# One kernel, one change: the first double by eight plain products, with both of its convolutions first

## The reference

```python
out = lax.conv_general_dilated(x, weight, window_strides=(STRIDE,), padding=[(PAD, PAD)], dimension_numbers=('NCH', 'OIH', 'NCH'), feature_group_count=GROUPS)
ctx = jnp.einsum('nd,od->no', c, c_weight)
out = out + ctx[:, :, None] + bias[None, :, None]
...
w = kernel.astype(x.dtype) * 2.0 - 1.0
return scale * jnp.einsum('bsi,if->bsf', x, w)
...
x = x + _L0_ffn_ref(_L0_cond_ref(x, cond_128, L0_cond_weight, L0_cond_c_weight, fside_S_0), L0_ffn_kernel, L0_ffn_scale)
```

## Time and profile before

| | us |
|---|---|
| median of 3 runs | 186.67 (186.43 to 186.93) |
| the profiled execution | 187.07 |
| its span in the trace | 185.0 |
| outside the span | 2.07 |
| PE busy | 171.9 (93%) |
| DVE busy | 132.3 (72%) |
| ACT busy | 69.0 (37%) |

### The profile page before, as it was taken

How to read it: one execution, slowest core, us unless ns; L and a number is a source line. 1 busy time by engine, 2 the same in 40 slices (tenths; PEclk the granted TensorE clock), 3 DMA queues, 4 the chain that set the end, 5 groups by cost and what they waited for, 6 DMA issues and landing times.

```text
span 185.0 us, 2886 instructions
## 1 busy us (share of the span) xinstructions
PE 171.9 (93%) x1007; PEld 148.8 (80%) x1007; DVE 132.3 (72%) x196; ACT 69.0 (37%) x77; POOL 6.6 (4%) x16
## 2 busy tenths in 40 slices
PE   3899799588999999999999999999999999999892
PEld 0569599376898989898899889888989889987681
DVE  4434788999967596758767786768766876587762
ACT  3534722491726163514624190617260502023000
POOL 5213200000000000000000000000000000000000
PEclk9999999999999999999999999999999999999999
DMA  6789785628696768376937785678834760005005
GB/s 221 186 201 299 208 246 83 150 39 153 137 287 148 170 100 319 70 177 97 265 118 111 164 167 230 88 170 113 315 56 59 103 238 5 0 0 227 4 0 227
DMA packets 23854, 27.51 MB, mean 149 GB/s; under 512 B 2753, under 2 KB 19313, under 8 KB 23841
## 3 DMA queue, kind: packets, MB, share of 16 engines
q1 hardware_dynamic: 22896, 25.96, 56.5%
q0 software_dynamic: 304, 1.09, 2.4%
q10 hardware_dynamic: 640, 0.28, 0.7%
HBM read 10.47 MB, written 8.40 MB: 102 GB/s over the span
## 4 chain that ended last, share of the span: by engine, by line
PE 87%; DVE 4%; DMA 3%; issue 3%; ACT 1%; ACTq 1%; DVEq 0%
PE ps_A L628 30%; PE ps_conv L610 30%; PE ps_C L628 15%; PE ps_B L628 8%; DMA cw_nat<-c_weight 3%; PE ps_A L577 2%; DVE sums L459 1%; PE ps_toep L628 1%; PE ps_C L597 1%; DVE y_sum L442 1%; DVE sign_T L415 1%; ACT hi_S L362 1%; DVE x_nat L480 0%; DVE lo_S L467 0%; ACT hi_A L362 0%
## 5 line engine op out<-in xcount | busy, mean ns | idle before, releaser
L610 PEld LDWEIGHTS ps_conv<-toeplitz,x_blk 128*128 128x128 f32 x512 | 61.2, 196 | 3.0 <-issue 1.9
L610 PE MATMUL ps_conv<-toeplitz,x_blk 128*128 128x128 f32 x512 | 61.3, 280 | 1.2 <-DVE y_sum L442 1.2
L362 ACT CAST hi_S<-sums 128x512 fp32r<-128x512 f32 x32 | 19.1, 621 | 55.5 <-DVE sums L459 54.7
L442 DVE TENSOR_TENSOR y_sum<-ps_conv,shift 128x512 f32<-128x512 f32 (+1 forms) x33 | 22.1, 674 | 18.2 <-PE ps_conv L610 11.4
L480 DVE SCALAR_TENSOR_TENSOR x_nat<-ps_A,scale_col,x_nat 128x512 f32<-128x512 f32 x31 | 23.2, 750 | 12.2 <-PE ps_A L628 12.1
L349 ACT COPY x_phase<-x_nat 128x1032 f32<-128x1032 f32 x13 | 28.2, 2173 | 0.0
L362 ACT CAST hi_A<-y_sum 128x512 fp32r<-128x512 f32 x24 | 14.0, 617 | 34.7 <-DVE y_sum L442 34.7
L467 DVE TENSOR_TENSOR lo_S<-sums,hi_S 128x512 fp32r<-128x512 f32 x32 | 21.8, 683 | 0.8 <-ACT hi_S L362 0.8
L628 PE MATMUL ps_A<-sign_T,hi_S 128*128 128x512 f32 x64 | 18.6, 412 | 1.8 <-DVE x_nat L480 0.9
L628 PE MATMUL ps_A<-sign_T,lo_S 128*128 128x512 f32 x64 | 17.1, 389 | 0.0
L467 DVE TENSOR_TENSOR lo_A<-y_sum,hi_A 128x512 fp32r<-128x512 f32 x24 | 16.3, 682 | 0.4 <-ACT hi_A L362 0.4
(11 more groups left out here) (68 smaller groups left out, 153.9 us busy)
## 6 DMA issues: line engine op xcount, KB each, us to landing
x_nat<-x SPq DMA_DIRECT2D x16, 512.0 KB, 4.1
x_blk<-x_phase SPq DMA_DIRECT2D x123, 64.5 KB, 2.5
out<-x_nat SPq DMA_DIRECT2D x15, 512.0 KB, 5.3
w_bytes<-w_bool SPq DMA_DIRECT2D x2, 512.0 KB, 5.9
shift<-shift_dram POOLq DMA_DIRECT2D x1, 896.0 KB, 5.7
out<-x_nat SPq DMA_DIRECT2D x1, 256.0 KB, 2.9
out<-x_nat SPq DMA_DIRECT2D x2, 128.0 KB, 2.8
x_blk<-x_phase ACTq DMA_DIRECT2D x3, 64.5 KB, 3.8
```

Of the source, the lines that this page charges most:

```text
L362: nc.scalar.copy(hi[k][:, :, :], flat(operand(k))).then_inc(hi_ok[k], 1)
L442: nc.vector.tensor_tensor(y_sum[r][:, u, a, :].rearrange("m u a o -> m a u o"), ps_conv[:, a, u, :], shift_of(d, r, a).unsqueeze(2).to_bro ...
L610: now = nc.tensor.matmul(ps_conv[:, a].rearrange("m u o -> m (u o)"), x_blk[r][:, a, s:s + M], toeplitz[:, s, g].rearrange("r u o -> r u ( ...
```

## The change

The first double is computed by eight plain products (`PLAIN`), with no S and no T operand. Both its convolutions come ahead of them; the convolutions of the second double stand behind the fifth and the seventh (`CONV_AFTER`). A21 shares its tiles with S4 and B12 with T4; a fourth bank E is the one that the Toeplitz transposes used. The steps 1 to 7 are as before on PE; T4 is now made ahead of step 1. B21 is made on ACT in four pieces that are signalled one by one. The sign bytes are loaded behind the first blocks of both pairs, where the first half stood ahead of them. The blocks of pair 1 are issued by three queues instead of one. DVE spreads all of the taps, whose load is now the third on ACT's queue. The shift of the first eight batches is one matmul of ones against `early_rows`, behind the first half of `conv(0, 0)`. `WARM` is 10 at the start and 2 ahead of the convolution. (Steps that count doubles only change their count; they are left out below.)

```diff
-WARM = 4, 3, 4
+WARM = 10, 2
...
-FIRST_BLOCKS = {("SP", 0): (0, 1), ("ACT", 0): (2, 3), ("SP", 1): (4,), ("ACT", 1): (5,), ("POOL", 1): (6, 7)}
-EARLY = 4
+FIRST_BLOCKS = {("SP", 0): (0, 1), ("ACT", 0): (2,), ("POOL", 0): (3,), ("SP", 1): (4,), ("ACT", 1): (5, 6),
+                ("POOL", 1): (7,)}
+EARLY = 8
...
+PLAIN = (("A12", "B21", "A"), ("A12", "B22", "B"), ("A22", "B21", "C"), ("A22", "B22", "E"), ("A11", "B11", "A"),
+         ("A11", "B12", "B"), ("A21", "B11", "C"), ("A21", "B12", "E"))
+CONV_AFTER = {4: 0, 6: 1}
+LAST_USE = {"A12": 2, "A22": 4, "A11": 6, "A21": 8}
+PLAIN_SUMS = {"A": (0, 0), "B": (0, 1), "C": (1, 0), "E": (1, 1)}
+PLAIN_BANK = {"P2": "B", "P1": "A", "P5": "C"}
+PLAIN_DONE = {"A": 5, "B": 6, "C": 7, "E": 8}
...
+        hi["A21"], lo["A21"] = hi["S4"], lo["S4"]
...
+        signs["B12"] = signs["T4"]
...
+        bank["E"] = ps_last[:, 0]
...
+            first_blocks(sp, "SP", 0)
+            first_blocks(sp, "SP", 1)
             signs_in(sp, 0)
-            first_blocks(sp, "SP")
+            load(1, 0, x_first[2])
             signs_in(sp, 1)
-            load(1, 0, x_first[2])
-            to_blocks(0, 1)
             load(1, 1, x_first[3])
...
-            first_blocks(pool, "POOL")
+            first_blocks(pool, "POOL", 0)
+            first_blocks(pool, "POOL", 1)
...
-            act.dma_start(taps_nat[:, :, :], weight).then_inc(taps_in, 16)
             act.dma_start(cond_nat[:, :], cond).then_inc(small_in, 16)
             act.dma_start(cw_nat[:, :], c_weight).then_inc(small_in, 16)
+            act.dma_start(taps_nat[:, :, :], weight).then_inc(taps_in, 16)
...
-            act.wait_ge(taps_zero, 1)
-            act.wait_ge(taps_in, 16)
-            expand_taps(nc.scalar.copy, B // 2, B).then_inc(exp_ok, 1)
...
+            first_blocks(act, "ACT", 1)
+
+            def sign(k, pieces):
+
+                rows = 0 if k[1] == "2" else KH
+                f = int(k[2]) - 1
+                for piece in range(pieces):
+                    n = KH // pieces
+                    u = KH - n * (piece + 1)
+                    nc.scalar.activation(signs[k][:, u:u + n, :], w_bytes[:, rows + u:rows + u + n, f * BANK:(f + 1) * BANK],
+                                         ACT.Copy, bias=-0.5, scale=1.0).then_inc(sign_ok[k], n)
...
-            high_part("A12", 0)
-            high_part("A11", 0)
-            sign("B22", slice(0, KH), 1)
-            to_phases(1, 1)
-            high_part("S2", 0)
-            high_part("S1", 0)
-            doubles(step)
+            def first_double():
+
+                high_part("A12", 0)
+                act.wait_ge(w_in[0], 16)
+                sign("B21", KH)
+                sign("B22", 1)
+                high_part("A22", 0)
+                high_part("A11", 0)
+                act.wait_ge(w_in[1], 16)
+                sign("B11", 1)
+                to_phases(1, 1)
+                sign("B12", 1)
+                high_part("A21", 0)
+                to_phases(2, 0)
+                high_part("A12", 1)
+                high_part("A11", 1)
+                to_phases(2, 1)
+                high_part("S1", 1)
+                high_part("S2", 1)
...
+            nc.vector.memset(warm[:, :], 0.0).then_inc(warm_ok, 1)
...
+            for half in range(2):
+                expand_taps(nc.vector.tensor_copy, half * B // 2, (half + 1) * B // 2).then_inc(exp_ok, 1)
...
-            dve.wait_ge(toep_done, 2)
-            toeplitz_of(nc.vector.tensor_copy, 1).then_inc(toep_ok, 1)
             dve.wait_ge(x_first[1], 16)
             nc.vector.tensor_copy(x_phase[1][:, :, 0:M + 1],
                                   x_nat[:, 1, :].rearrange("r (m q) -> r q m", q=B)).then_inc(phase_ok[1], B)
+            dve.wait_ge(toep_done, 2)
+            toeplitz_of(nc.vector.tensor_copy, 1).then_inc(toep_ok, 1)
+            dve.wait_ge(ctx_done, 1)
             dve.wait_ge(bias_in, 16)
-            dve.wait_ge(ctx_done, 1)
-            nc.vector.tensor_tensor(shift_rows[:, :], ps_ctx, bias_rows[0:N, :], ALU.add).then_inc(shift_ok, 1)
+            nc.vector.tensor_tensor(shift_rows[:, :], ps_ctx, bias_rows[:, :], ALU.add).then_inc(shift_ok, 1)
+            dve.wait_ge(shift_ok, 1)
+            dve.wait_ge(ident_ok, 1)
+            nc.vector.tensor_tensor(early_rows[:, :, :], shift_rows[:, :].unsqueeze(1).to_broadcast([N, EARLY, C]),
+                                    ident[0:N, 0:EARLY].unsqueeze(2).to_broadcast([N, EARLY, C]), ALU.mult
+                                    ).then_inc(rows_ok, 1)
             dve.wait_ge(early_done, 1)
-            nc.vector.tensor_tensor(shift[:, 0:EARLY // 2].rearrange("m j a o -> m (j a o)").rearrange("m (n o) -> m n o", n=EARLY),
-                                    ps_early.rearrange("m (n o) -> m n o", n=EARLY),
-                                    bias_rows[:, :].unsqueeze(1).to_broadcast([P, EARLY, C]), ALU.add).then_inc(early_ok, 1)
+            nc.vector.tensor_copy(shift[:, 0:EARLY // 2].rearrange("m j a o -> m (j a o)"), ps_early).then_inc(early_ok, 1)
...
+            def plain_sum(b):
+
+                r, f = PLAIN_SUMS[b]
+                dve.wait_ge(plain_done, PLAIN_DONE[b])
+                there = line(0, r, *columns(f))
+                nc.vector.scalar_tensor_tensor(there, bank[b], scale2_col[:, :], there, ALU.mult, ALU.add
+                                               ).then_inc(plain_summed[b], 1)
+
+            def first_double():
+
+                LOW, HIGH = slice(0, KH // 2), slice(KH // 2, KH)
+                add_shift(0, 0, 0)
+                add_shift(0, 0, 1)
+                low_part("A12", 0)
+                add_shift(0, 1, 0)
+                add_shift(0, 1, 1)
+                dve.wait_ge(scale_in, 16)
+                nc.vector.tensor_scalar(scale2_col[:, :], scale_col[:, :], 2.0, 0.0, ALU.mult, ALU.add
+                                        ).then_inc(scale_ok, 1)
+                low_part("A22", 0)
+                low_part("A11", 0)
+                for half in range(2):
+                    dve.wait_ge(w_in[half], 16)
+                sign_sums("T3", w_bytes[:, 0:KH, BANK:L], ALU.subtract, w_bytes[:, KH:B, BANK:L])
+                low_part("A21", 0)
+                dve.wait_ge(sign_ok["T3"], KH)
+                dve.wait_ge(sign_ok["B11"], KH)
+                sign_sums("T2", plain("T3"), ALU.add, plain("B11"))
+                dve.wait_ge(scale_ok, 1)
+                plain_sum("A")
+                dve.wait_ge(sign_ok["T2"], KH)
+                dve.wait_ge(sign_ok["B22"], KH)
+                sign_sums("T1", plain("B22", LOW), ALU.subtract, plain("T2", LOW), LOW)
+                add_shift(1, 0, 0)
+                sign_sums("T1", plain("B22", HIGH), ALU.subtract, plain("T2", HIGH), HIGH)
+                add_shift(1, 0, 1)
+                plain_sum("B")
+                low_part("A12", 1)
+                plain_sum("C")
+                low_part("A11", 1)
+                add_shift(1, 1, 0)
+                add_shift(1, 1, 1)
+                for k in ("S1", "S3", "S2", "S4"):
+                    combine(k, 1)
+                plain_sum("E")
+                low_part("S2", 1)
+                dve.wait_ge(sign_ok["B21"], KH)
+                dve.wait_ge(plain_done, LAST_USE["A21"])
+                for u in (LOW, HIGH):
+                    sign_sums("T4", plain("B21", u), ALU.subtract, plain("T2", u), u)
...
-            for n in range(EARLY):
-                now = nc.tensor.matmul(ps_early[:, n * C:(n + 1) * C], cond_t[:, n:n + 1].to_broadcast([D, P]), cw_t[:, :],
-                                       start=True, stop=True)
-            now.then_inc(early_done, 1)
-            keep_busy(WARM[2])
+            keep_busy(WARM[1])
+
+            def early_shift():
+
+                pe.wait_ge(ones_ok, 1)
+                pe.wait_ge(rows_ok, 1)
+                nc.tensor.matmul(ps_early, ones[:, :], early_rows[:, :, :].rearrange("k n o -> k (n o)"),
+                                 start=True, stop=True).then_inc(early_done, 1)
...
+            def first_double():
+
+                for n, (of, k, b) in enumerate(PLAIN):
+                    pe.wait_ge(hi_ok[of], 1)
+                    opens = n < 4
+                    for part in (hi, lo):
+                        if part is lo:
+                            pe.wait_ge(lo_ok[of], 1)
+                        for u in range(KH):
+                            if part is hi:
+                                pe.wait_ge(sign_ok[k], u + 1)
+                            now = nc.tensor.matmul(bank[b], part[of][:, u, :], signs[k][:, KH - 1 - u, :],
+                                                   start=opens and u == 0 and part is hi,
+                                                   stop=not opens and u == KH - 1 and part is lo, skip_group_check=True)
+                    now.then_inc(plain_done, 1)
+                    if n in CONV_AFTER:
+                        conv(1, CONV_AFTER[n])
...
```

(18 more changed lines are left out.)

221 lines of the change are left out of this document (94 added, 127 removed).

## The result

The changed kernel takes 181.38 us in the median of 4 runs (180.59 to 181.48), the kernel before 186.80 us in the same comparison: ratio 0.9698, 95% interval 0.9663 to 0.9733. A second set of six runs gave 181.65 us (181.31 to 182.18), ratio 0.9736 (0.9710 to 0.9762). So the change is 3.0% or 2.6% faster, 5.2 to 5.4 us. The forecast was 179.8 us, the range 178.0 to 182.6.

The account below looks back on a forecast made before the run. PE bounds the kernel, with holes before step 1, where DVE's queue is tight. Step 1 at 40.5 + 0.4 + 0.3 = 41.2 instead of 48.07, 6.9 us less: 180.2 profiled, 179.8 median; range 178.0 to 182.6.

Parts of the forecast that it names:

- The case that it rested on: Whole kernel: the prediction's own sum, 179.8 us, holds within 0.8 us; chance 0.45.
- the sum of a rival: Slow-clock rival: light work before the first convolution brings the slow clock back; step 1 at 42.9, 181.5 us; chance 0.20.
- Start: Before the first convolution: taps land at 6.6, are spread and transposed; convolution starts at 10.8 us, 2.8 us earlier.
- Sum of the work: First convolution to step 1 on PE: four convolutions, eight products and the early shift take 29.74 us without a wait.
- Clock: First convolution: counted at full speed, as ten matmuls on zeros precede it; the slow clock had cost 1.66 us before.
- Sign bytes: First products: bytes land at 16.8 us (15.3 to 17.8); the second product waits 0.4 us for B22.
- DVE behind low_part of A21: First double: T2, T1 and sums queue on DVE; convolution (1, 1) does not wait, with 1.0 us left.
- DVE or ACT becomes the bound: First double: ACT slips 1.5 to 2.5 us, PE waits at convolution (1, 1) and P6; 181.5 to 182.5 us; chance 0.20, later start included.
- P6 of step 1: Start of step 1: P6 waits for bank A's sum, last of 12.0 us of DVE work; counted +0.3 us.
- Blocks of the convolution (1, 0): First double: blocks land by 27.5 us, wanted at 28.2 and 30.0; hidden by less than a microsecond.
- The first sign bytes: Rival, slower than before: bytes land 7 us later, at 24 us, holding up all products; chance 0.02.
- Queues give more: Rival at the start: taps land at 5.6, sign bytes at 15.3; step 1 at 39.8, 178.4 us; chance 0.11.

Follow-up runs that it names:

- e6: The changed kernel with one matmul on zeros at the start in place of ten: 181.39 us.
- e8: The changed kernel with T4 made at its old, later place and T2 made twice on DVE (2.28 us more work): 180.88 us.
- e9: The changed kernel with T2 made twice on DVE, T4 still ahead of step 1: 182.68 us.
- e1: The changed kernel with four more matmuls on zeros between the two small transposes and the sixteen: 181.60 us.
- e2: The changed kernel with T4 made at its old place, behind low_part(A22, 1), instead of ahead of step 1: 181.04 us.
- e11: The changed kernel with sign block B21 made in one piece instead of four: 181.03 us.
- e4: The kernel before (seven products in the first double) with the new start and both convolutions first: 186.20 us.
- e7: The changed kernel with T4 at its old place, twelve matmuls on zeros at the start and three between small transposes and the sixteen: 180.25 us.
- e10: As e7, with the first sign bytes issued between the blocks of pair 0 and those of pair 1: 180.32 us.

## Why the prediction came out as it did

The forecast stood: the time lies in the range and moved as forecast, 5.4 us of the 6.9 expected. The case that it rested on did not: both medians lie 1.6 us and more above 179.8, and the sum of a rival came true. Step by step:

- **Start.** First convolution expected at 10.8, measured at 9.98 and 10.46. The taps landed at 6.1 (taken: 6.6, bounds 5.6 and 7.8), 4.3 us after their issue and so between the two cases weighed, and the transposes took 1.4 in place of 1.94 where the clock was up.
- **Sum of the work.** 29.74 expected from the first convolution to step 1; in the trace with 8 slow records it is 31.45, in that with 16 it is 32.14. The second closes as 29.74 + 1.76 (the first half, 3.55 against 1.79) + 0.49 (the early shift, 1.39 against 0.90) + 0.14 (the first two products); the first as 29.74 + 0.97 + 0.16 + 0.31 + 0.26, the last for blocks. The early shift took 1.05 (0.90 expected) at the full clock. The four convolutions and eight products at their unit prices are right: from the third product at 23.12 to step 1 at 41.43 it is 18.31, where six products and two convolutions make 18.05.
- **Clock.** This is the term that was mis-sized. I took the convolution at full speed and gave the slow clock a chance of 0.20. Of the ten profiles with the new start and eight products, only the two with twelve and three matmuls on zeros had no slow record; the eight others had 5 to 16, among them both of the changed kernel. The rival's own sum was 181.5 with step 1 at 42.9; measured 181.4 and 181.65, with step 1 at 42.60 in the trace that stands for the median. So the number that came true is the rival's, and so is the slow first half under it. That the two sums meet so well is in part luck: the rival has the first convolution at 11.2 (10.46 measured) and the early shift at 0.90 (1.39), and these two cancel but for 0.2. What I had taken as proof against it, ten dense matmuls instead of four, is refuted by e6: one gives the same median. How the slow clock came about is only in part as the rival had it. In four profiles (both of the changed kernel, e8, e9) the granted clock came up at 4.5 to 6.3 us and was back at half from 7.9 to 9.7 us on, behind the light work. In three others with the same ten matmuls (e1, e2, e11) the transposes were slow already, and the clock came up only at 13.3 to 14.1.
- **Sign bytes.** Taken at 16.8, landed at 17.02. With the fast start product 2 began at 21.19, behind B22 (done at 21.0 expected, 21.05 in the trace). Product 1 had begun at 19.18, so without a wait product 2 could have begun at 21.0: the wait was 0.2 and not 0.4. With the slow clock it was covered, as the rival's sum had it.
- **DVE behind low_part of A21.** Slack of 1.0 expected, 2.4 there: the second half of `add_shift(1, 0)` was done at 35.34 (36.1 expected), and the half of the convolution that needs it started at about 37.8 (37.1 expected). e8 puts 2.28 us into it and waits 0.2. So the rival "DVE or ACT becomes the bound" does not stand, although 181.5 to 182.5 holds one of the two medians: PE has no wait in the first double of either trace beyond the ones named here.
- **P6 of step 1.** +0.3 expected, 0.37 measured (3.86 against 3.49), by the cause named; e2 takes it away. The prediction's own sum gives nothing here (48.1 against 48.1), so the 0.3 was an allowance and its size is luck.
- **Blocks of the convolution (1, 0).** Expected to be hidden by under a microsecond, issued from about 18 and landed by 27.5. In the first trace they were issued from 20.73 and the last landed at 29.59; the weight load of that convolution waited 0.39 us for them, and PE lost some 0.26 (18.31 against 18.05). In the second trace they landed at 27.5 and cost nothing. e4 shows 2.4 us as soon as the cover of three products is gone.
- **Steady part.** 136.9 us behind step 1 expected; 178.8 - 41.43 = 137.4, which is the same and the wait of P6.
- **Rivals that fell.** The first sign bytes never came near 24 us. "Queues give more" did not come: the taps were early and the bytes were not.

Open: why the clock comes up and stays in one execution and not in the next. Twelve and three matmuls on zeros, with no pause over 0.4 us ahead of the convolution, gave two profiles of two without a slow record; two are few. The missing pause is not enough to explain it: e1, with ten and four, had none over 0.4 us either, and its clock came up only at 13.3.

## What to carry to other kernels

A form with fewer products can lose to the plain one in the first tile: what the saved product asks for (sums of operands, sums of signs, both halves of a load) is made while nothing else covers it. Here eight products with both convolutions first were 3.3 us faster on the same start, the 1.8 us of extra matmul already paid. Changes to a start are not additive: the same earlier start gave 1.9 to 2.1 us with this form and order and cost 1.8 with the old ones, where the sign bytes, moved behind the blocks, held up the first product by 3.1. So test a start with the form that it serves. Before you count on a dense stretch to bring the clock up, look at the durations of the first real matmuls in more than one profile.

## What the runs showed that I had not expected

- **The clock at the first real matmul is a draw.** The same kernel had 8 slow convolution records of 421 ns in one execution and 16 in another, with 1.2 us between the two at step 1. The Trainium skill (TensorE: Matmul & The Clock Gate, Part 1) says that the number of slow matmuls varies from run to run of the same kernel; the traces agree. It also puts the penalty under 1% of a typical span. The two executions differ by 180.59 against 181.74 us, 0.6%; neither had its whole first half at the full clock, so this is not the whole penalty. Against a change of 3% it is a fifth, so it decided here where in the range the time fell.
- **The granted clock of a page may miss the first stretch.** The mean granted clock of the e1 profile is 1.00 and its row has a 9 in every slice, and yet 8 of its convolution records took 421 ns. The first profile has as many, but there the row shows them (the 6, and 0.99 in the mean). The durations are the measure.
- **A fuller start and an earlier load trade one wait for another.** With the clock up (e7) the sign bytes were late, with the bytes at 13.7 (e10) the blocks of pair 1 were, at up to 16.4: first product at 19.18 and 19.36. In these two profiles it is transfers that hold this start up once the clock is up; no run had both early.
